# A decoder layer on one core: the output projection of cross attention, the feed-forward part and the last layernorm in 14 tiles of 128 tokens in place of 16 batches of 112

## The reference, cut to what matters

```python
x1 = layernorm(x  + self_attention(x))           # 16 heads of 16, causal
x2 = layernorm(x1 + cross_attention(x1, ctx))    # 375 keys, the last step is out @ w_o.T
g, u = fp4_linear(x2, w_gate), fp4_linear(x2, w_up)   # 256 -> 704 each, inputs and weights
                                                      # quantised in blocks of 16
y  = layernorm(x2 + fp4_linear(silu(g) * u, w_down))  # 704 -> 256
```

## Time and profile before

| what | value |
|---|---|
| median of 3 runs | 662.46 us (661.29 to 663.1) |
| the profiled execution: its own time | 661.05 us |
| the profiled execution: span of its instructions | 659.2 us |
| instructions | 16222 |
| mean granted TensorE clock | 0.97 of full speed |
| DMA | 67.78 MB |

### The profile page before, as it was taken

One profiled execution on the slowest core, in us unless ns is written; L12 is line 12 of the kernel. 1 busy time (PEld: TensorE's weight loads), 2 busy tenths in 40 slices (PEclk: granted clock), 3 DMA queues, 4 the chain that ended last, 5 costly groups with the idle time before them and its releaser, 6 DMA issues.

```text
span 659.2 us, 16222 instructions
## 1 busy us (share of the span) xinstructions
PE 592.7 (90%) x5682; PEld 380.1 (58%) x5682; DVE 509.9 (77%) x1555; ACT 294.6 (45%) x717; POOL 213.8 (32%) x286
## 2 busy tenths in 40 slices
PE   3687798899999999999999999999999999997964
PEld 3445465566666666666666656665666665553532
DVE  3679688896978869696968687887969696979772
ACT  1144354445454555454545455454545454442411
POOL 5244234315150524242341515051424233223001
PEclk9789899899999999999999999999999999999996
DMA  6734461515252433526251525343342512120000
GB/s 168 212 95 138 140 191 49 175 32 150 75 152 86 132 107 74 164 56 178 54 143 59 158 70 151 87 133 106 91 148 59 173 50 88 49 88 2 9 7 14
DMA packets 64464, 67.78 MB, mean 103 GB/s; under 512 B 11696, under 2 KB 55936, under 8 KB 64384
## 3 DMA queue, kind: packets, MB, share of 16 engines
q1 hardware_dynamic: 64384, 66.75, 35.1%
HBM read 39.72 MB, written 27.00 MB: 101 GB/s over the span
## 4 chain that ended last, share of the span: by engine, by line
PE 64%; DVE 20%; issue 8%; ACT 3%; POOL 3%; SPq 1%; DMA 1%; DVEq 0%; POOLq 0%; ACTq 0%
PE misc L2020 18%; PE prob L1960 7%; PE misc L2101 6%; PE misc L2041 5%; PE xpv L2001 5%; PE misc L2012 5%; PE score L1946 5%; DVE junk L1262 4%; PE prob L1955 4%; DVE amax L1254 2%; PE apv L1989 2%; PE misc L2054 2%; PE misc L2062 2%; DVE qt L1176 2%; DVE hq L1180 1%
## 5 line engine op out<-in xcount | busy, mean ns | idle before, releaser
L1262 DVE CUSTOM_DVE_ANT_0 junk<-score,maskbias 112x375 bf16<-112x375 f32 x256 | 128.5, 540 | 43.3 <-PE score L1946 42.8
L800 ACT ACTIVATE xP<-prob 128x448 f32<-128x448 f32 (+1 forms) x192 | 98.5, 542 | 106.8 <-PE prob L1960 106.5
L638 POOL TENSOR_TENSOR rstd<-veps,half 112x1 f32<-112x1 f32 x48 | 27.2, 576 | 295.9 <-DVE veps L1340 295.9
L2020 PE MATMUL misc<-wguT,xqT 128*112 128x352 f32 x256 | 87.2, 468 | 0.5 <-ACT xqT L764 0.5
L633 POOL TENSOR_TENSOR move_a<-mT,negeye 16x448 bf16<-16x448 f32 x64 | 60.6, 969 | 77.9 <-ACT mT L764 77.9
L633 POOL TENSOR_TENSOR move_x<-mT,negeye 16x448 bf16<-16x448 f32 x64 | 65.3, 1036 | 53.9 <-ACT mT L764 53.9
L2020 PEld LDWEIGHTS misc<-wguT,xqT 128*112 128x112 f32 x256 | 44.2, 180 | 24.6 <-issue 2.9
L1960 PE MATMUL prob<-move_x,shift_x 128*128 128x448 bf16 x192 | 54.0, 360 | 1.5 <-POOL move_x L633 1.4
L2020 PE MATMUL misc<-xwvT_s,ctxT_s 128*128 128x256 f32 (+1 forms) x192 | 52.2, 395 | 0.0
L2101 PE MATMUL misc<-wdT,hqT 128*112 128x256 f32 x192 | 49.6, 402 | 1.5 <-ACT hqT L764 1.5
L1946 PE MATMUL score<-xK,xQ 64*128 64x375 f16 x256 | 42.9, 329 | 6.7 <-DVE xmax L1262 6.2
(11 more groups left out here) (163 smaller groups left out, 1117.5 us busy)
## 6 DMA issues: line engine op xcount, KB each, us to landing
xk_dram<-xk_parts SPq DMA_DIRECT2D x64, 192.0 KB, 3.1
xK<-xk_dram SPq DMA_DIRECT2D x16, 768.0 KB, 4.6
ctxT_s<-in_ctxT SPq DMA_DIRECT2D x16, 375.0 KB, 3.8
aq_dram<-aq_parts SPq DMA_DIRECT2D x64, 64.0 KB, 2.6
ak_dram<-ak_parts SPq DMA_DIRECT2D x64, 64.0 KB, 2.1
aQ<-aq_dram SPq DMA_DIRECT2D x16, 256.0 KB, 3.6
aK<-ak_dram SPq DMA_DIRECT2D x16, 256.0 KB, 2.8
xq_dram<-xq_parts SPq DMA_DIRECT2D x64, 64.0 KB, 2.1
```

What stands on the lines that cost most here:

```text
L800: act.activation(xP[0:KEYS[c], g % 2, c], prob[m][0:KEYS[c], 0:GH * S].rearrange("p (h q) -> p h q", h=GH), ACT.Exp).then_inc(probs.taken[ ...
L1262: dve.tensor_tensor_reduce(junk[:, m], score[m][0:S, 0:SC], maskbias[:], 1.0, -3.0e38, ALU.add, ALU.max, xmax[:, b.par, h:h + 1]).then_inc ...
L2020: mm = pe.matmul(misc[m][0:rows_, 0:cols], actT(c), weightT(c), start=(c == 0), stop=(c == DT - 1))
```

## The change

Cross output projection, its residual and layernorm, the feed-forward part, the last layernorm and the store work on 14 tiles of 128 tokens. Attention, the self output projection and the first layernorm stay with 16 batches of 112.

- xattT, the transposed attention output, becomes a ring of 7 x 128 = 8 x 112 columns. Batches write 112 columns, a tile reads 128, once the two or more batches that it touches are there.
- The rows of x1 for the second residual are written by GpSimd to x1rows and go from there by DMA (`put_x1`, new, on SP) to their rows in x1kept, now four tiles of 128 rows. A batch that crosses a tile border needs two transfers.
- Buffers of the tiled part are 128 partitions high. The transposes of the tiled part use an identity of 128 columns in place of 112.
- `tile(slot)` gives the tile of a slot. Slots 3 to 9 have the gate and up of tiles 0 to 6, slot 10 of none, slots 11 on of tiles 7 on. `f = tile(i)`, `ft = tile(i - 1)` (down, last layernorm), `xo = tile(i + 1)` (output projection). Before it was f = i-2, ft = i-3, output projection i-1. So the ramp now holds slots -2 to 3, and slot 2 has no feed-forward work; in slot 10 gate and up are missing, in slot 11 down, in slot 9 the cross output projection. The drain has the tiles 10 to 13 where it had the batches 12 to 15.
- The lists of calls of all five engines are laid out anew, in the ramp, the slot and the drain. In the slot TensorE projects X.o after X.mT instead of before x1's transpose, and v before the gate; GpSimd's keep_x1 goes from before the cross diagonals to after the second and the power of the cross layernorm; SP's next_ctx goes to the end. In the drain, the down projection of the last tile but one stands behind the gate and up of the last.

The diff, cut to its core (the lists of calls of ramp and drain are left out but for one piece):

```diff
+TILES = B * S // P
+RING = 7
-FIRST, LAST = 3, 13
+FIRST, LAST = 4, 13
+def tile(slot):
+    t = slot.c - 3 if slot.c < 10 else slot.c - 4
+    return Batch(t) if slot.c != 10 and 0 <= t < TILES else None
+def tile_slot(t):
+    return Batch(t + 3 if t < 7 else t + 4)
+def pieces(t, second):
+    n = 0
+    for b in range(B):
+        first, row = b * S // P, b * S % P
+        if (not second and first <= t) or (second and row + S > P and first + 1 <= t):
+            n += 1
+    return n
...
-        xattT = sb("xattT", [P, DT, S])
+        xattT = sb("xattT", [P, DT, RING * P])
-        x1kept = sb("x1kept", [S, 3, D])
+        x1rows = sb("x1rows", [S, 2, D])
+        x1kept = sb("x1kept", [P, 4, D])
...
+            def put_x1(b):
+                t, row = b.c * S // P, b.c * S % P
+                n = min(S, P - row)
+                sp.wait_ge(kept, b.times(1, 1))
+                sp.nop(nofuse=True)
+                for second in range(2):
+                    wait_if(sp, kept_in[second], 16 * sum(1 for c in range(b.c) if not second or c * S % P + S > P))
+                    sp.nop(nofuse=True)
+                wait_if(sp, x_ready[1], t - (3 if n == S else 2))
+                sp.nop(nofuse=True)
+                sp.dma_start(x1kept[row:row + n, t % 4], x1rows[0:n, b.par]).then_inc(kept_in[0], 16)
+                if n < S:
+                    sp.dma_start(x1kept[0:S - n, (t + 1) % 4], x1rows[n:S, b.par]).then_inc(kept_in[1], 16)
...
             def residual_cross(i, b):
-                dve.wait_ge(kept, b.times(1, 1))
-                add_residual(i, 1, "X.o", x1kept[:, b.c % 3])
+                for second in range(2):
+                    wait_if(dve, kept_in[second], 16 * pieces(b.c, second))
+                    dve.nop(nofuse=True)
+                add_residual(i, 1, "X.o", x1kept[:, b.c % 4])
...
+            def project_cross(i, b):
+                if b.c == 0:
+                    pe.wait_ge(w_xo, 16)
+                    pe.nop(nofuse=True)
+                for c in range(b.c * P // S, (b.c * P + P - 1) // S + 1):
+                    miscs.wait_taken(pe, Batch(c + 1), "X.att")
+                    pe.nop(nofuse=True)
+                lo = b.c % RING * P
+                project_rows(i, "X.o", lambda c: xattT[:, c, lo:lo + P], lambda c: xwoT_s[:, c], P, D)
...
# GpSimd, slot
                 diagonal(i, a, 3, False)
+                if ft:
+                    power(2, ft)
+                    shifts(2, ft)
                 residual(a)
                 power(0, a)
-                power(2, ft)
                 shifts(0, a)
-                shifts(2, ft)
-                keep_x1(a)
                 diagonal(i, c, 0, True)
                 diagonal(i, c, 1, True)
-                power(1, ct)
+                if xo:
+                    power(1, xo)
+                keep_x1(a)
                 diagonal(i, c, 2, True)
...
# TensorE, slot
                 front(i, fr, "k")
-                gate_up(i, f, "gate", 0)
+                front(i, fr, "v")
                 turned_self(i, a, 0)
-                gate_up(i, f, "up", 0)
-                front(i, fr, "v")
+                if f:
+                    gate_up(i, f, "gate", 0)
+                    gate_up(i, f, "up", 0)
                 scores_cross(i, c, 0)
...
                 turn_att(i, "X", 1)
-                ctx_v(i, kv, 2)
-                project_out(i, ct, "X", xattT, xwoT_s)
+                ctx_v(i, kv, 1)
                 turn_x1(i, a)
                 turn_max(i, c, "X.mT", xmax)
-                ctx_v(i, kv, 1)
+                if xo:
+                    project_cross(i, xo)
                 project(i, "A.q", xwqT_s, x1T, S, after=("A.xT",))
...
# TensorE, drain, its end
+                project_cross(at[16], at[13])
+                turn_hq(at[17], at[12], "hT1", range(4, IC))
+                turn_hq(at[17], at[12], "hT0", range(4))
+                turn_xq(at[17], at[13])
+                gate_up(at[17], at[13], "gate", 0)
+                gate_up(at[17], at[13], "up", 0)
+                gate_up(at[17], at[13], "gate", 1)
+                gate_up(at[17], at[13], "up", 1)
+                down(at[17], at[12])
+                turn_hq(at[18], at[13], "hT1", range(4, IC))
+                turn_hq(at[18], at[13], "hT0", range(4))
+                down(at[18], at[13])
```

More of the change, by code:

```diff
@@ L111, in par @@
         return self.c % 2
-def steady(order):
-    return [(i, label) for i in range(FIRST, LAST + 1) for label in order]
+def tile(slot):
[3 more added lines that the diff above has]
+    return Batch(t + 3 if t < 7 else t + 4)
+TILED = {"X.o": 1, "X.xT": 0, "gate0": 0, "up0": 0, "gate1": 0, "up1": 0, "hT0": -1, "hT1": -1, "down": -1}
+def steady(order):
+    return [(i, label) for i in range(FIRST, LAST + 1) for label in order
+            if label not in TILED or tile(Batch(i + TILED[label]))]
+def pieces(t, second):
[5 more added lines that the diff above has]
+    return n
 class Ring:
@@ L671, in ramp @@
                 keep_x1(at[0])
+                residual(at[1])
                 residual(at[2])
@@ L1002, in slot @@
+                turned_weight("dn1")
+                ctxv(at[3], at[4], 2)
+                layernorm(at[4], 0, x1[:, at[4].par])
+                ctxv(at[3], at[4], 1)
+                take(at[3], "A.xT", x1T[:])
+                maxima(at[3], 1, "X.mT")
+                xq_hi_(at[3], at[4])
             def slot(i):
```

1623 lines of the change are left out of this document (891 added, 732 removed), and 21 rows, old and new, of tables (MISC_IN, MISC_OUT, SCORE_IN).

## The result

| what | before | after |
|---|---|---|
| median in the comparison (20 runs each) | 663.37 us (661.29 to 665.74) | 658.49 us (654.18 to 663.99) |
| ratio, 95% interval | | 0.9922 (0.9901 to 0.9943) |
| profiled execution, span | 661.05, 659.2 us | 658.93, 657.1 us |

The changed kernel is 0.8% faster, 5 us where 20 were forecast, and outside the range of 634 to 652. Its runs spread over 10 us, those of the kernel before over 4.5.

A forecast was written before the change was run, and what follows sets the result against it. TensorE was taken to bound steady slots, TensorE and VectorE nearly full in the ramp, a dependent chain in the tail. -19.6 + 0.5 + 2.2 - 1 - 2 = -19.9 us; median forecast 643 us, range 634 to 652.

The forecast's parts named there:

- ramp -10.8 forecast: Up to slot 4's self-maxima transpose: one feed-forward pass leaves, 9.8 us, and 1 us more from VectorE's relief.
- slots with the hole -7.6 forecast (-9.8 + 2.2): Slots 9 to 11: one pass leaves, 9.8 us of TensorE, against 2.2 us of new waits, bounds 0 and 5.
- drain -2 forecast: Drain: the last-but-one down moves behind the last gate into a 5.94 us TensorE gap; -2 us, bounds +3 and -5.
- Work taken from TensorE in a steady slot comes back one for one: Steady slots: TensorE busy 349.75 of 358.2 us, so each microsecond removed there was taken to shorten the kernel equally.
- the term 2 x 9.8 = 19.6: Sixteen feed-forward passes become fourteen, one fewer in the ramp, one in slots 9 to 11; 9.8 us of TensorE each.
- (a to c): New waits, slots 9 to 11: second diagonal 0.7 us, cross scores in slot 10 1.0, query round trip 0.5.
- the ramp does not shorten at all: Ramp: VectorE's weight work sets its length, kernel 653 us; part of the rival that new waits eat much, chance 0.17.
- a gain not taken (2.6 us): Drain: with the idle gap half filled, the last down might keep full clock, giving 2.6 us more; not counted.
- The walk: New order followed engine by engine with recorded prices; 0.7 us of waits kept per slot, drain put at -2 us.
- the kept rows: Residual rows' DMA before residual_cross: forecast to cost nothing; landing late was the mechanism of the slower rival, 678 us, chance 0.03.
- Slot 10 near 31: Sign of being right: slot 10 takes near 31 us, the named waits included; slots 4 to 9 take 35.2 to 36.
- the signs of being wrong: TensorE waits above 75 us, residual_cross waiting for a DMA, or steady slots off 35.5 by over half a microsecond.

The follow-up runs named there:

- run 9: Kernel before with batch 8's gate, up and down matmuls (middle) cut to 8 columns, that part of the computation left out: 661.96 us, ratio 0.9976.
- run 13: Kernel before with batch 0's feed-forward matmuls in the ramp cut to 8 columns and 19 unread matmuls put in the ramp's holes: 663.36 us, ratio 1.0001.
- run 8: Changed kernel with unread matmuls in three tail waits, plus 26 in the ramp and 13 in slot 11: 652.28 us, 0.9821 to the kernel before.
- run 7: Changed kernel with the slot without feed-forward moved from slot 10 to slot 3: 655.06 us, 0.9864 to the kernel before.
- run 4: Changed kernel with 33 unread matmuls ahead of three waits in the tail: 652.82 us, 0.9850 to the kernel before.
- run 6: Kernel before with 31 unread matmuls in its tail, 4 ahead of the last input transposes, 27 ahead of the last hidden-row transposes: 661.26 us, ratio 0.9959.
- run 14: Changed kernel with hole in slot 3, old drain, early context and filled tail, plus 15 unread matmuls in slot 4: 645.93 us, 0.9738 to the kernel before.
- run 5: Changed kernel with the drain in the old order and batch 15's context asked for early: 652.01 us, 0.9823 to the kernel before.
- run 15: Changed kernel with hole in slot 3, old drain, early context, filled tail; slot 4 takes self maxima before the quantiser, input transposes later: 650.70 us, 0.9803.
- run 16: As run 15, but VectorE takes the query's low half before the quantiser and the key's low half before its last three steps: 651.52 us, 0.9807.
- run 1: Changed kernel with the drain in the old order on all five engines, context request left at the list's end: 666.19 us, 1.0023 to the kernel before.
- run 10: Kernel before with batch 0's gate, up and down matmuls (ramp) cut to 8 columns, that part of the computation left out: 666.56 us, ratio 1.0043.

## Why the prediction missed

The forecast was some 15.5 us too low. Its terms against the traces (the ramp by the means above): ramp -10.8 forecast, -7.1 measured; slots with the hole -7.6 forecast (-9.8 + 2.2), -1.9 measured; drain -2 forecast, +5.2 measured. The misses are 3.7, 5.7 and 7.2 us; the full slots, 0.7 us shorter in sum, and the 0.5 for transposes, which does not show, give back 1.2.

1. **"Work taken from TensorE in a steady slot comes back one for one", and so the term 2 x 9.8 = 19.6.** This is the step that failed, and with it the drain's term (4). A full share of busy time said that TensorE was the bound; it did not say what the other chains would need once it was shorter. In the middle 5.1 us cut gave 1.6 (run 9), in the ramp nothing even with the clock back at its usual share (run 13), and the whole pass left out at slot 10 gave 1.9 of 9.8. Of the rest 4.7 became waits and 1.6 went to the lower clock (38.7 us for 37.1 with the waits filled, run 8); the last 1.6 are work of TensorE in slot 10 that by the record did not get shorter by as much as was taken out, and are not explained. Behind the hole it is the chain from the output projection through VectorE to the quantised input, 9.7 us, that the transposes of the hidden rows and the down had hidden. The prediction had cases for a missing query, score banks and diagonals (a to c) and never asked this of the quantised input. The sum for the waits in slots 9 to 11 was 2.2 us, bounds 0 to 5; 4.7 more than in full slots came, near the upper bound. The forecast cases make up 1.0 of it (0.31 at the diagonals, 0.64 at a score bank, nothing at the query), the self maxima and the quantised input 3.9.
2. **The ramp.** Forecast 9.8 + 1 us; the cut of slot 4 moved 4.7 in the profiled pair, from 193.7 to 189.0, and 7.1 by the means. In the pair TensorE's busy time there fell by 6.2 and waits rose by 1.5. With the hole inside the ramp's end (run 7) another 4.9 us go from the ramp, and 4.7 come back in slots 4 to 12, 3.2 of them in slot 4 as waits and lower clock. The rival "the ramp does not shorten at all" was too strong, its direction right.
3. **The granted clock had no price.** The prediction counted it only as a gain not taken (2.6 us). In the changed kernel TensorE's clock stands at the lower level for some 57 us, before for some 40 (mean clock 0.957 and 0.970). The tail alone lost 4.8 us by it (run 4) against 2.7 before (run 6), and the hole 1.6 more (runs 8 and 14).
4. **The drain: -2 forecast, +5.2 in the trace.** The walk looked at one down and its gap, and priced the other moves of the lists at nothing. The order costs 6.6 us (run 5). The down in the gap was no gain: VectorE had the last hidden rows 12.4 us after the last gate's start where it had taken 11.2, and two holes ahead of the last gate replaced part of the one behind it. Yet this walk saw only the end: some two thirds of the loss arise before the last output projection. Which of the drain's moves costs most was not taken apart.
5. **Right:** the passes left (224), full slots at 35.5 us, so that 128 rows cost nothing that can be seen against 112; the kept rows, for which residual_cross waits nowhere; and the sign. Slot 10 near 31 (30.8) came out too, but the price stood in slot 11, 38.7 us, which no case had: that hit alone says little. Of the signs of being wrong one came true, 75.4 us of waits for a limit of 75. By an estimate from the Trainium skill's rule on weight loads ("TensorE: Matmul & The Clock Gate", section "LDWEIGHTS (loading the stationary operand)") exposed loads would have added 6.0 us over the tiles, some 0.4 in a slot; the trace, 35.5 before and after, does not show them.

What stays open: in the middle, 3.05 of 4.35 us became waits at full clock in small pieces (0.92 us at a score bank, 1.41 at the quantised input and others), and it was not shown which chain sets the pace there. That VectorE's chain holds the slot behind the hole is read from its waits and from two orders that only moved them (runs 15 and 16); no run made the chain itself shorter. In the early ramp the clock falls at times that differ between executions of equal code, and filling gave nothing there that the times can tell.

## What to carry to other kernels

A busy share of 98% does not say what a microsecond less is worth: cut the columns of some matmuls in one place, leave all else, and read the time. This probe costs one kernel and would have put the main term here to the test. When work is taken out at one place, ask which chain of another engine it was hiding, from its first producer on, which of that chain's steps will now run beside another engine's, and price the clock with it. Short waits in a tail can be filled with matmuls that nobody reads, and lists written out by hand for two stages must be tried together: the old drain lost 13 us only because the new slot loads its context last. Compare a stretch with several traces of equal code before it is called shorter: the pair of profiles here had 4.7 us for the ramp where the means have 7.1, and the 9 us of slot 3 in run 7 were in part a later start.

## What the runs showed of the hardware

- TensorE's clock fell behind two waits of 1.28 and 2.04 us with a microsecond of work between them, and stood at 0.5 for 3.4 us. With 13 unread matmuls in these waits (run 8) or 15 in the like ones (run 14) it did not fall.
- It stays low for a while when work is back: in run 1 TensorE was full from 550 on and had a clock of 0.68 over the next 5 us.
- One recorded instruction of a float32 matmul takes 0.12 us with 8 columns (0.47 for four), 0.34 with 352 (1.35 for four): 44 times fewer columns gave a third of the time.
- Two VectorE steps of two float32 inputs (128x256) took 1.04 us each beside GpSimd's diagonals, 0.42 without (changed kernel, 433.39 and 434.46 us, against 330.55 and 331.01; likewise in runs 7 and 14, and one such step in run 9). Side by side is what the rows show; no run separates the two.
- Less work can be slower. Cutting 5.1 us of matmuls lost 2.9 us in the ramp, and 19 unread matmuls won them back (runs 10 and 13).
